# Two-queue setup loads, a combination without copies, and new turn tables in a one-core adaLN / Mamba / soft-MoE kernel

## What is computed

```python
mod = (silu(c) @ wmod).reshape(8, 6, 1, -1)          # sa, ca, ga, sb, cb, gb of each sequence
h = layernorm(x) * (1 + ca) + sa
x = x + ga * mamba(h)       # rmsnorm, in_proj, 4-tap conv, silu, softplus(dt), scan, silu(z) gate, out_proj, + h
h = layernorm(x) * (1 + cb) + sb
x = x + gb * soft_moe(h)    # logits to 8 x 64 slots, two softmaxes, 8 experts (gelu), combination
...
out = einsum('bmd,bnm->bnd', eo, combine)            # combine: softmax of the logits over the 512 slots
```

## Time and profile before

| | us |
|---|---|
| median of 3 runs | 254.81 (254.8 to 255.49) |
| the profiled execution | 255.61 |
| its span | 253.6 |
| PE busy | 221.5 (87%) |
| DVE busy | 146.6 (58%) |
| ACT busy | 138.1 (54%) |
| POOL busy | 48.3 (19%) |
| matmuls / DVE / ACT / POOL instructions | 1161 / 450 / 284 / 91 |

### The profile page before, as it was taken

One profiled execution on the slowest core, in us unless ns is written; L12 is line 12 of the kernel. 1 busy time (PEld: TensorE's weight loads), 2 busy tenths in 40 slices (PEclk: granted clock), 3 DMA queues, 4 the chain that ended last, 5 costly groups with the idle time before them and its releaser, 6 DMA issues.

```text
span 253.6 us, 3444 instructions
## 1 busy us (share of the span) xinstructions
PE 221.5 (87%) x1161; PEld 143.2 (56%) x1161; DVE 146.6 (58%) x450; ACT 138.1 (54%) x284; POOL 48.3 (19%) x91
## 2 busy tenths in 40 slices
PE   4818996999779877998999779997999999998895
PEld 3506463766537576636767547785445445454894
DVE  2484879687889999778787787551020111102243
ACT  5246699652055685799732156576818154360451
POOL 6152920001462467000001550000000000000000
PEclk9965799799999999999799889999999999999999
DMA  6303000200060000000500000000022230500022
GB/s 196 79 0 131 0 3 0 87 0 4 0 179 29 3 0 3 0 3 0 166 6 0 0 0 4 0 3 0 0 83 83 71 97 0 165 1 0 23 80 65
DMA packets 13632, 9.90 MB, mean 39 GB/s; under 512 B 1598, under 2 KB 11943, under 8 KB 13615
## 3 DMA queue, kind: packets, MB, share of 16 engines
q1 hardware_dynamic: 12798, 9.16, 12.3%
q10 hardware_dynamic: 816, 0.52, 0.7%
HBM read 8.56 MB, written 1.07 MB: 38 GB/s over the span
## 4 chain that ended last, share of the span: by engine, by line
PE 61%; DVE 23%; ACT 7%; issue 3%; POOL 2%; DMA 2%; SPq 2%; DVEq 0%; ACTq 0%
PE bank L537 52%; DVE xcT L1275 3%; PE bank L665 3%; DVE hh L1203 2%; DVE bst L1133 2%; DVE cmax L1373 2%; DVE rmax L1364 2%; DVE hh L1195 2%; DMA vec_nat<-ffn_slot_norm_gamma_dram 2%; PE bank L760 2%; POOL root L486 1%; DVE xntok L1229 1%; PE bank L860 1%; DVE BT L1388 1%; PE bank L806 1%
## 5 line engine op out<-in xcount | busy, mean ns | idle before, releaser
L1413 DVE SCALAR_TENSOR_TENSOR seg_e<-bank,vecT,gbT 128x512 f32<-128x512 f32 x8 | 6.0, 751 | 54.1 <-PE bank L537 54.1
L537 PE MATMUL bank<-slotsT,w_sb 128*128 128x512 f32 x64 | 28.2, 593 | 0.8 <-issue 0.8
L537 PE MATMUL bank<-eo,xhT 128*128 128x129 f32 (+1 forms) x192 | 24.0, 282 | 4.1 <-DVE xhT L1347 3.3
L537 PE MATMUL bank<-xnT,winT 128*128 128x512 f32 x48 | 25.3, 660 | 1.5 <-ACT CTr L990 1.0
L537 PEld LDWEIGHTS bank<-eo,xhT 128*128 128x128 f32 x192 | 22.8, 195 | 5.6 <-DVE xhT L1347 3.7
L1074 ACT ACTIVATE zsT<-bank,vecT 128x512 f32<-128x512 f32 x16 | 11.0, 687 | 21.0 <-PE bank L537 20.9
L537 PEld LDWEIGHTS bank<-slotsT,w_sb 128*128 128x128 f32 x64 | 12.1, 190 | 15.9 <-issue 14.4
L1275 DVE SCALAR_TENSOR_TENSOR xcT<-bank,convw,xcT 128x510 f32<-128x510 f32 (+2 forms) x24 | 17.7, 738 | 5.7 <-ACT xcT L979 5.7
L486 POOL TENSOR_TENSOR root<-root,neg_half 128x2 f32<-128x2 f32 (+1 forms) x24 | 20.2, 842 | 2.0
L1019 ACT ACTIVATE seg_e<-bank 128x512 f32<-128x512 f32 x24 | 12.6, 604 | 14.1 <-PE bank L537 14.1
L481 POOL TENSOR_SCALAR root<-mv 128x2 f32<-128x2 f32 (+1 forms) x12 | 4.0, 334 | 84.6 <-DVE mv L1136 84.6
(11 more groups left out here) (167 smaller groups left out, 427.6 us busy)
## 6 DMA issues: line engine op xcount, KB each, us to landing
w_sb<-in_L_ffn_w_dram SPq DMA_DIRECT2D x16, 256.0 KB, 3.1
mods_bc<-mod_dram SPq DMA_DIRECT2D x4, 320.0 KB, 3.7
xin<-in_L_attn_x_dram SPq DMA_DIRECT2D x4, 256.0 KB, 3.1
out_dram<-xin SPq DMA_DIRECT2D x8, 128.0 KB, 1.8
mods_bc<-mod_dram SPq DMA_DIRECT2D x4, 192.0 KB, 3.2
eo<-in_L_attn_in_proj_w_dram SPq DMA_DIRECT2D x1, 384.0 KB, 3.9
eo<-n_L_ffn_slot_embeds_dram ACTq DMA_DIRECT2D x1, 256.0 KB, 5.5
eo<-in_L_wmod_dram SPq DMA_DIRECT2D x1, 256.0 KB, 5.7
```

What stands on the lines that cost most here:

```text
L537: return nc.tensor.matmul(o, lhsT, rhs, start=start, stop=stop)
L1413: V.scalar_tensor_tensor(eoT[:, :, j, :], bank[4 + j][:, :].rearrange("p (b s) -> p b s", b=B), vecT[:, bass.ds(it * 2 + (RB2 + j), 1)], g ...
```

## The change

1. **Transfers.** The six vectors and the dt rows are issued by ACT instead of SP, right after the tanh. The slot embeddings and out_proj are issued by SP instead of ACT, last in the setup. The dt rows have a semaphore of their own, `s_dt`.
2. **First modulation rows.** The "1 +" is one bf16 matmul for each half (of `ident_b`, whose first column is summed) instead of one fp32 matmul for each sequence. PE makes the rows of half 0, then transposes the vectors, w and the dt rows, and makes those of half 1 after that.
3. **Turns.** All tables get new numbers. The squares of the slot embeddings become a `once` step. `small_rows` signals (`ACT_SMALL`), and two consumers wait for it.
4. **Combination.** PE reads `combT` directly; ACT's eight copies are gone. For sequences 0 and 1 the first three chunks are multiplied as soon as the last transposes of the experts are issued, and only the fourth waits for the last copy of `eo`. The result is written over `x1tok` and sent from there, so DVE no longer waits for `y_sent`.

```diff
@@ SP
-            for r0, n, src in vecs:
-                sp.dma_start(vec_nat[r0:r0 + n, :], src).then_inc(s_vec, 16)
-
-            sp.dma_start(dt_nat[:, :], in_proj_w[DT0:ROWS, :]).then_inc(s_wo, 16)
             sp.dma_start(convw[:, :, :], conv_w.rearrange("(c p) k -> p c k", p=P)).then_inc(s_small, 16)
...
+            sp.dma_start(se_nat[:, :, :],
+                         slot_embeds.rearrange("(n a) s d -> (a s) n d", a=P // S)).then_inc(s_se, 16)
+            sp.dma_start(wo_nat[:, :], out_proj_w).then_inc(s_wo, 16)
...
-            pipeline(sp, [((4, 3, 6, 7), next_x), ((2, 1, 8, 9), next_mods), ((0, 5, 10, 11), send_parts)])
+            pipeline(sp, [((3, 4, 5, 7), next_x), ((2, 1, 8, 9), next_mods), ((0, 6, 10, 11), send_parts)])
...
-                                 yout[j][:, 0:NT, :]).then_inc(y_sent[1][j], 16)
+                                 x1tok[:, of_batch(it * 2 + j), :]).then_inc(y_sent[1][j], 16)
@@ PE
-            one_row = ident[:, 0:1].broadcast_to((P, P))
-            for j in range(2):
+            pe.wait_ge(s_pool, POOL_IDENT_B)
+            one = ident_b[:, 0:1]
+
+            def first_mods(j):
+                o = bank[5 + j][:, :].rearrange("p (b m d) -> p b m d", b=BP, m=2)
                 for bi in range(BP):
-                    b, o = j * BP + bi, bank[5 + j][:, 2 * bi * P:2 * (bi + 1) * P]
-                    mm(o, cs[:, b:b + 1].broadcast_to((P, P)), wmod_sb[:, 0:2 * P], stop=False)
-                    q = mm(o[:, P:2 * P], ones_sq[:, :], one_row, start=False)
-                q.then_inc(s_pe0, 1)
+                    b = j * BP + bi
+                    nc.tensor.matmul(o[:, bi, :, :].rearrange("p m d -> p (m d)"), cs[:, b:b + 1].broadcast_to((P, P)),
+                                     wmod_sb[:, 0:2 * P], start=bi == 0, stop=False, skip_group_check=True)
+                nc.tensor.matmul(o[:, :, 1, :], one.broadcast_to((P, P)), one.unsqueeze(1).broadcast_to((P, BP, P)),
+                                 start=False, stop=True, skip_group_check=True).then_inc(s_pe0, 1)
+
+            first_mods(0)
             pe.wait_ge(s_vec, N_VEC)
...
-            pe.wait_ge(s_wo, N_WO)
+            pe.wait_ge(s_dt, 16)
             nc.tensor.transpose(bank[2][:, 2 * P:2 * P + H], dt_nat[:, :], ident[0:H, 0:H]).then_inc(s_pe0, 1)
+            first_mods(1)
...
+            def combine(b, chunks):
+                j, it = b % 2, b // 2
+                for n in range(NT):
+                    for m in chunks:
+                        q = mm(bank[2 * j + n][:, 0:P + 1], combT[:, b, m, tile_cols(n)], eo[:, b, m, :],
+                               start=m == 0, stop=m == MT - 1)
+                    if m == MT - 1:
+                        q.then_inc(comb_out_ps[1][j], 1)
+
+            pe.wait_ge(eo_done, E - 2)
+            pe.wait_ge(s_eo_ones, 1)
+            for b in range(2):
+                combine(b, range(MT - 1))
             pe.wait_ge(eo_done, E)
...
+            for b in range(2):
+                combine(b, [MT - 1])
+            for b in range(2, B):
+                wait_before(pe, y_out, b % 2, b // 2)
+                combine(b, range(MT))
@@ ACT
-            act.dma_start(se_nat[:, :, :],
-                          slot_embeds.rearrange("(n a) s d -> (a s) n d", a=P // S)).then_inc(s_se, 16)
-            act.dma_start(wo_nat[:, :], out_proj_w).then_inc(s_wo, 16)
+            act.dma_start(dt_nat[:, :], in_proj_w[DT0:ROWS, :]).then_inc(s_dt, 16)
...
+            for r0, n, src in vecs:
+                act.dma_start(vec_nat[r0:r0 + n, :], src).then_inc(s_vec, 16)
...
-            def copy_comb(j, it):
...
-                    wait(act, comb_out_ps, j, it)
-                    copy_comb(j, it + 1)
@@ DVE
-            visits = [((0, 3, 53, 57), statistics1), ((2, 4, 54, 59), centre1), ((6, 5, 58, 60), modulate1),
+            visits = [((0, 3, 52, 58), statistics1), ((1, 4, 54, 59), centre1), ((2, 7, 55, 61), modulate1),
...
-            pipeline(dve, visits, once=[(1, vectors), (7, rows_of_mods), (9, gate_columns)])
+            pipeline(dve, visits, once=[(6, vectors), (8, rows_of_mods), (9, gate_columns)])
...
-                    wait_before(dve, y_sent, j, it)
...
-                        q = V.scalar_tensor_tensor(yout[j][:, n, :], bank[2 * j + n][:, 0:P], rden[j][:, n:n + 1],
...
+                        q = V.scalar_tensor_tensor(x1tok[:, t, :], bank[2 * j + n][:, 0:P], rden[j][:, n:n + 1],
+                                                   x1tok[:, t, :], ALU.mult, ALU.add)
```

More of the change, by code:

```diff
@@ L570, in t_wo @@
                 pe.wait_ge(s_dve0, DVE_ROWS)
+                pe.wait_ge(s_wo, 16)
                 for k in range(CT):
@@ L696, in visit @@
                     wait(pe, dtx_done, j, it, bi + 1)
+                    if it == 0:
+                        pe.wait_ge(s_act0, ACT_SMALL)
                     for k in range(CT):
@@ L821, in _ @@
                       ((55, 58, 115, 118), shifts(1)), ((57, 61, 117, 119), fill_slots(1)),
-                      ((60, 64, 120, 121), t_slots(1))]
-            pipeline(pe, visits, once=[(0, t_wo), (2, t_slot_embeds)])
+                      ((60, 66, 120, 121), t_slots(1))]
+            pipeline(pe, visits, once=[(1, t_wo), (4, t_slot_embeds)])
             for j in range(2):
@@ L872, in _ @@
             t_outputs(E // 2 - 1)
-            pe.wait_ge(eo_done, E)
-            pe.wait_ge(s_eo_ones, 1)
-            for it in range(B // 2):
-                for j in range(2):
-                    wait(pe, cb_done, j, it)
-                    wait_before(pe, y_out, j, it)
-                    for n in range(NT):
-                        for m in range(MT):
-                            q = mm(bank[2 * j + n][:, 0:P + 1], cbuf[j][:, m // 2, (m % 2) * L + n * P:(m % 2) * L + n * P + P],
-                                   eo[:, bass.ds(it * 2 + j, 1), m, :].rearrange("p b d -> p (b d)"),
-                                   start=m == 0, stop=m == MT - 1)
-                        q.then_inc(comb_out_ps[1][j], 1)
+            def combine(b, chunks):
[10 more added lines that the diff above has]
+                combine(b, range(MT - 1))
+            pe.wait_ge(eo_done, E)
+            for b in range(2):
[3 more added lines that the diff above has]
+                combine(b, range(MT))
         @block.scalar
@@ L906, in _, with slot_squares @@
             rsm_rows(0)
-            act.wait_ge(s_se, 16)
-            for m in range(MT):
-                A(se_sq[:, :], se_nat[:, m, :], ACT.Square, scale=float(DM) ** -0.5, accum_out=se_ss[:, m:m + 1]).then_inc(s_act0, 1)
-                act.wait_ge(s_act0, ACT_TANH + m + 1)
+            def slot_squares():
+                act.wait_ge(s_se, 16)
+                for m in range(MT):
+                    A(se_sq[:, :], se_nat[:, m, :], ACT.Square, scale=float(DM) ** -0.5,
+                      accum_out=se_ss[:, m:m + 1]).then_inc(s_act0, 1)
+                    act.wait_ge(s_act0, ACT_SE - MT + m + 1)
             def scale_win():
@@ L942, in small_rows @@
                 for k in range(CT):
-                    A(diag_d[:, k, :], ident[:, :], ACT.Identity, scale=d_col[:, k:k + 1])
+                    q = A(diag_d[:, k, :], ident[:, :], ACT.Identity, scale=d_col[:, k:k + 1])
+                q.then_inc(s_act0, 1)
             def mods(j, it, bi):
@@ L1059, in _ @@
[L1059 to L1066 removed]
+            visits = [((0, 4, 52, 56), mean_squares1), ((2, 12, 61, 67), copy_xnT), ((6, 14, 63, 69), exp_dt),
+                      ((7, 15, 64, 70), first_tap), ((8, 16, 65, 71), copy_c), ((18, 17, 66, 72), silu_z(0)),
+                      ((21, 19, 73, 74), silu_z(1)), ((22, 20, 76, 75), silu_x(0)), ((23, 25, 77, 78), silu_x(1)),
+                      ((24, 27, 80, 79), copy_scores), ((26, 28, 81, 82), copy_parts), ((29, 33, 83, 86), decay(0)),
+                      ((30, 34, 84, 88), decay(1)), ((31, 35, 85, 91), decay(2)), ((32, 38, 87, 93), decay(3)),
+                      ((36, 39, 89, 94), decay(4)), ((37, 40, 90, 95), decay(5)),
+                      ((41, 42, 92, 98), mean_squares2(0)), ((43, 47, 96, 100), mean_squares2(1)),
+                      ((44, 48, 97, 102), copy_xn2T(0)), ((45, 49, 99, 103), copy_logits(0)),
+                      ((46, 50, 101, 104), copy_xn2T(1)), ((51, 53, 105, 106), exps(0)),
+                      ((54, 57, 107, 109), copy_logits(1)), ((55, 58, 108, 110), copy_slotsT(0)),
+                      ((59, 60, 111, 112), exps(1)), ((62, 68, 113, 114), copy_slotsT(1))]
@@ L1068, in gelus @@
+            pipeline(act, visits, once=[(1, scale_win), (3, slot_squares), (5, unit_slots), (9, small_rows),
+                                        (10, copy_wo), (11, copy_sn), (13, lambda: rsm_rows(1).then_inc(s_act0, 1))])
             def gelus(it):
@@ L1083, in _ @@
             gelus(0)
-            for j in range(2):
-                copy_comb(j, 0)
             for it in range(E // 2 - 1):
@@ L1089, in _ @@
             copy_eo(E // 2 - 1)
```

(4 more changed lines are left out.)

109 lines of the change are left out of this document (46 added, 63 removed).

## The result

| | before | after |
|---|---|---|
| median of the runs, us | 254.81 (4 runs, 254.65 to 255.49) | 259.00 (4 runs, 257.61 to 260.56) |
| profiled execution, us; its span | 255.61; 253.6 | 259.04; 257.3 |
| mean granted clock in it | 0.953 | 0.960 |

The ratio is 1.018, with a 95% interval of 1.014 to 1.022: **slower, by 4.2 us**, where 5.8 us faster was forecast. Medians hold all executions of a kernel; ratios leave out those more than 1.5% above its fastest.

The account below looks back on a forecast made before the run. DVE idle 3.3 us in the setup behind the vectors' load, then ACT from 34.00 to 45.74, then PE and DVE were the bounds. 5.0 at the first segment plus 0.8 in the combination took 254.81 to 249.0; range 246.7 to 251.6.

Parts of the forecast that it names:

- The setup: From the start to the first conv tap on DVE: tap at 22.0 instead of 26.43, 4.4 us earlier.
- come at the same absolute time: no term: Setup: mod_rows ready about when it was, so mods_bc and POOL's long additions keep their absolute time; counted as no term.
- The ACT block: From half 1's exponential (30.9) to the first segment: ksm0 ends 9.0 later, ksm1 at 41.4; first segment 5.0 us earlier.
- under 4 us: Sign set beforehand: a gain at the first segment below 4 us would mean the mechanism was wrong.
- The same instructions ... I take 0 for it, with 0.7 either way: From 43 us to the combination: same instructions on nearly full engines, last turns in the same sequence; 0 gain, 0.7 either way.
- The combination: Last stage: two waits go, sequence 2 waits 0.45 us; gain 0.8 us, ends 0.2 and 1.3.
- The dense stage starves PE: Rival, slower: half 0's second y ahead of half 1's first costs about 3.5 us in each pass, 256.1; chance 0.05.
- The other queue does not help the vectors: Rival, setup: vectors land only 0.26 us earlier, at 9.0, everything behind moves by 1.1, 250.1; chance 0.13.

Follow-up runs that it names:

- again: The changed kernel unaltered, run once more beside the others: 258.82 us, ratio 1.018 to the kernel before.
- pool_late: The changed kernel with POOL's additions of the first pass held until half 1's softplus is through: 253.91 us, ratio 0.994 to the kernel before.
- softmoe_old: The changed kernel with the order of before from the first pass's second norm on, second pass included: 253.38 us, ratio 0.993 to the kernel before.
- order_only: The kernel before with the new order from the parts on and in the second pass: 257.65 us, ratio 1.011 to the kernel before.
- norm_old: The changed kernel with the order of before from the first pass's second norm to the second pass's running sums: 255.13 us, ratio 1.002 to before.
- filler: The changed kernel with four idle PE multiplications in the wait ahead of the first pass's logits: 256.77 us, ratio 1.009 to the kernel before.
- before_filler: The kernel before with idle PE multiplications in the wait ahead of the logits, both passes: 253.75 us, ratio 0.999 to the kernel before.
- best_filler: softmoe_old with POOL's first-pass additions held until half 1's parts, plus four idle PE multiplications ahead of both passes' logits: 250.79 us, ratio 0.983 to before.

## Why the prediction was wrong

**The setup: right in size, and up to the modulation rows in mechanism.** 4.4 us was forecast at the first tap, 4.8 came. The vectors were ready at 8.50 (7.9 forecast, 9.0 the bound). The transposes of w took 1.54 us, near the 1.74 taken, though the profile gives the granted clock as 1.00 there. DVE did wait for `centre1` of half 1 (3.20 us, to 12.59; 12.2 forecast). `mod_rows` was copied at 16.00, and `mods_bc` landed at 24.8. The last steps went another way than forecast, and that 21.63 came so near 22.0 is in part luck. PE's dt products began at 17.54, with the granted clock at 1.00 up to 19 us, and were done at 18.5, where 19.5 was forecast. What ended last was ACT's and POOL's work on the slot embeddings and half 1's roots: ACT's first tap began at 20.69, right behind it, and DVE's tap stood behind half 1's scaling. The chain that ended last has, between 19 and 22 us:

```profile
19.76 1.05 POOL root L475
20.84 0.87 DVE xntok L1234 x4
```

**The step that failed first** is "come at the same absolute time: no term". The additions did come at the same time (24.82, before 25.04). But everything else had moved by 4.8 us, so the same additions now lay beside other work: before, beside the taps, the small steps between them and the first Horner steps; now, beside all six Horner steps and the four behind them. Conv and softplus of half 0 took 8.55 us before (26.43 to 34.98), 11.46 after (21.63 to 33.09) and 6.57 with POOL held back (22.36 to 28.93). That is a missing term of 2.9 us, and its sign could be read in the trace of before: L1259's six steps took 2.22 us in half 0, where POOL was at work, and 1.22 in half 1, where it was not. A row in which one instruction has two durations asked for a reason.

**The ACT block.** From half 1's exponential to the end of `ksm0` I had 9.0 us. With POOL out of the way it is 10.4 (29.26 to 39.68; ACT was busy for 9.64 of it, and I had no term for its waits). That the first segment came there at 42.30, where 43.1 was forecast, is two errors that cancel: the block took 1.4 more, and the exponential came 1.6 earlier than my 30.9, since without POOL beside it the softplus is also 2.0 shorter than in the kernel before. In the changed kernel the block was 11.8, since PE, idle for 2.93 us behind the slow softplus, did half 1's projections at clock 0.50, and ACT waited 2.09 us for them. Together: the gain at the first segment was 0.45, and the condition that I had set for being wrong in mechanism ("under 4 us") was met.

**"The same instructions ... I take 0 for it, with 0.7 either way"** failed too, by more. From half 0's first logits to the experts it is 104.64 before, 109.34 after, 109.29 in again. I had looked at the last turns of each pass and took their equal sequence for an equal order; the middle had been laid anew. The profile of pool_late has the same order with the upper clock in the two stages where the changed kernel fell, and takes 106.23. By it, 3.1 of the 4.7 us are PE's clock: two stretches at the lower level, worth 1.5 to 1.7 us each (7.06 against 5.61; 21.25 or 17.15 against 19.59 or 15.51). The other 1.6 are the order itself (2.3 against softmoe_old's 103.97): DVE's token maximum ahead of a scaling and PE's transposes laid to match in the logits (5.61 against 5.29 and 4.93), and the second pass's segments (52.4 to the experts; 51.6 before, 50.8 in softmoe_old). This split rests on single profiles, and pool_late's is one of its fastest runs. The total doesn't: order_only and softmoe_old show by their runs that the order, with what PE's clock does in it, costs 1.1% and 2.4%.

**The combination** was over-sized a little: 0.6 for 0.8. The 0.46 ahead of sequence 2 was there as forecast.

**The rivals.** "The dense stage starves PE" had the sign right and the place wrong: the first pass keeps half 0's second y where it was and loses nothing, and in the second pass the segments lose 0.5 us (norm_old) to 1.5 (the changed kernel) against softmoe_old, not 3.5. It had a chance of 0.05 for a table of turns of which I had costed one swap. In its place: two stages each lost about as much as the setup had won. "The other queue does not help the vectors" isn't settled: the last of them was issued 0.11 earlier than before (5.05, 5.16) and landed 0.73 earlier (8.50, 9.23), but two large loads had changed their place as well.

**Open.** Where PE's clock falls isn't explained. It isn't the order behind the wait: with the same wait ahead of the logits (1.62 or 1.63 us) the first group was slow in the changed kernel, in order_only and, with the order of before behind it, in softmoe_old, and fast in the kernel before, in norm_old and in pool_late. It isn't the amount either: the mean granted clock of the profiles is 0.953 before and 0.960 after, and the kernel before has its own low stretches (44 to 49, 120 to 124 and 144 to 148 us). filler shows that the wait takes part in it in the changed kernel; before_filler and best_filler show that filling it needn't gain anything. Each profile shows one execution only. A version without the contention at all (POOL's additions left out) wasn't run.

## What to carry to other kernels

When an early stage moves, list what does not move with it, and ask what it now lies beside: here POOL's work, tied to a transfer, ate 2.9 of 4.8 us without being waited for by anyone. If the same instruction has two durations in a trace, find the reason before summing. And a new order on in-order engines is costed step by step for every step that changes place, not by its first and last ones; a fall of PE's clock doesn't cost the same in every order: 0.3 us in one, 1.5 in the other.
